# Last four steps of a Mamba-2 scan beside the first gated products: the order of three engines' helper work

## Chip, cores and metric

The kernel runs on one core of a Trainium2 chip. The metric is the device time of one execution in microseconds (us): the median of the runs, and for a profiled execution also its span, from the first to the last instruction. Engines: TensorE (PE) multiplies, VectorE (DVE) and ScalarE (ACT) work elementwise, GpSimd (POOL) too, SyncE (SP) issues transfers.

## What is computed

One macaron block over 2048 tokens of width 512: half a quantised feed-forward with a LoRA part, a Mamba-2 layer followed by a gated MLP, half a feed-forward again. The part that matters here:

```python
x = x + 0.5 * ffn(layernorm(x))
res = h0 = layernorm(x)
h = res + mamba2(rmsnorm(h0, ln1_w), ...)        # scan over 16 chunks of 128 tokens, 4 heads
#   per chunk: att = (C @ B.T) * Ldec;  Y = att @ Xdt + C @ state * exp(cs) + D * x
#              state = exp(cs[-1]) * state + dec_end * B.T @ Xdt
#              y = Y * silu(z);  y @ w_out.T
h2 = rmsnorm(h, ln2_w)
mlp = (silu(h2 @ gate_w.T) * (h2 @ up_w.T)) @ down_w.T      # inner width 1792
x = x + h + mlp
x = x + 0.5 * ffn(layernorm(x))
```

## The kernel before

The program is written by hand for every engine; each runs its own list in order, and semaphores (`wait_ge`, `then_inc`) join them. Tokens are cut into 16 chunks of 128, named c here; CH is 4, so the last four scan steps are c = 12 to 15 (`3 * CH` to `3 * CH + 3` in `late_steps`, one such function on each of GpSimd, ScalarE and VectorE). The MLP's inner width is cut into 7 pairs of 256 columns.

**TensorE in step c** (L2452 on, `step`): the transposes of the next chunk, the chunk's diagonal product with S (L2391, waits for GpSimd's e_SD), the product with the state (L2401), two more for the next step, then one gate-and-up product (`gate_up`, 24 matmuls of 128x512 at L2295), then the output product `w(c)` (L2418, L2422, L2425). Gate products are numbered n = 0 to 7; n = 0 to 3 lie in steps 12 to 15. After step 15 come n = 4, with `bound_turn(1)` (L2466) between its two halves, `bound_spread(1)` (L2471), n = 5, `down(0)` (four products t = 0 to 3), n = 6, `down(1)`, n = 7, and then seven-product units (a Strassen scheme) for pairs 1 to 6. Product n = 4 overwrites the banks of n = 3 and waits for e_gated 4, VectorE's second gate instruction of n = 3 (L2119). The product t = 3 of `down(0)` overwrites a bank that holds the bounds and waits for e_wscale 2, which VectorE gives when pair 1's scales are made. The first unit's product IP6 waits for e_gated 8 (n = 7).

**ScalarE**: `high_y` (L885) copies y to its high half; `renorm` (L875) makes n1; `gate_a` (L1376) is the tanh of a gate; `gate_b` (L1381) the high half of a gated tile; `hi2(c)` (L870) the normed high half of chunk c, into the single buffer h2n_p, so that it waits for the transpose of chunk c - 1 (s_h2T) and for GpSimd's r2 (e_rms2); `square` (L889) sums squares; `t_his` (L1325) takes high halves of the Strassen sums; `norm` (L1276) folds pair 1's scales in, waiting for e_wscale; `st_a` (L1285 to L1293) makes its high halves.

**VectorE**: `gate_y` (L1649), `low_y` (L1658), `lo2(c)` (L1596, then SyncE transposes h2n_p, L484), `t_los` (L1787) the low halves of the sums, `gate_up` (L2118, L2119), `residual2` (L1674), `gate_lo` (L2125), `bound_g` (L1708) and `bounds` (L1712 to L1715) for pair 1's maxima, `bound_row` (L1722, L1723), `scale_read` and `scales` (L1730, L1499 to L1502, L1736).

**GpSimd**: `scan_c` (L612), `scan_d` (L616, L618), `rms2(c)` (L622, L586 and the accumulating transfer L625), and `sums(first, end)`: elementwise sums of 128x512, eight for each quarter q of the tokens (n // 8 is q). They are held in four buffers hn, h2n, n0_p, hn_p (called t1, t3, t2, t4). A sum of quarter q that overwrites one of them waits (`t_ready`) until VectorE has taken the low half of that buffer's sum of quarter q - 1 (e_tlo). After the sums of q = 2 come four adds `s_adds(1)` (L774 to L779), which wait for `norm`.

The rows of an execution name these lines; in the changed file all lines behind GpSimd's list stand 5 lower, so that L1376 is L1371 there.

Of the kernel before, what the change touches and what calls it, by code (L numbers as in the profile page):

```python
# [29 lines left out]
def build(nc, x_in, w_in_t, conv_w, conv_b, a_log, d_skip, dt_bias, w_out_t, ln1_w, ln2_w,  # L30
# [14 lines left out]
    CH = ST // P  # L45
# [8 lines left out]
    with ctx:  # L54
# [522 lines left out]
        def _(po):  # L577
# [29 lines left out]
            def scan_c(c, j):  # L607
                cols = slice(j * P, (j + 1) * P)
                s = (c // CH) % 2
                po.wait_ge(e_ecs, c + 1)  # L610
                po.wait_ge(e_G, c + 1)
                po.tensor_tensor(xbc[s][:, 2:CB, cols], xbc[s][:, 2:CB, cols], ecs[:, j % 2, :, :], ALU.mult).then_inc(e_Cdec, 1)  # L612
# [83 lines left out]
            def late_steps():  # L696
                for c in range(2 * CH, 2 * CH + 3):
                    scan_c(c + 1, (c + 1) % CH)
                    scan_d(c + 1, (c + 1) % CH)
                    rms2(c, c % CH)  # L700
                scan_c(3 * CH, 0)
                scan_d(3 * CH, 0)
                rms2(2 * CH + 3, 3)
                sums(0, 2)
                scan_c(3 * CH + 1, 1)
                scan_d(3 * CH + 1, 1)
                sums(2, 4)
                rms2(3 * CH, 0)
                scan_c(3 * CH + 2, 2)
                scan_d(3 * CH + 2, 2)  # L710
                sums(4, 6)
                rms2(3 * CH + 1, 1)
                sums(6, 8)
                scan_c(3 * CH + 3, 3)
                scan_d(3 * CH + 3, 3)
                sums(8, 11)
                rms2(3 * CH + 2, 2)
                sums(11, 16)
                rms2(3 * CH + 3, 3)
                sums(16, 20)  # L720

            def sums(first, end):
                for n in range(first, end):
                    t_op(n // N_TOP, n % N_TOP)
# [108 lines left out]
        def _(ac):  # L833
# [242 lines left out]
            def late_steps():  # L1076
# [82 lines left out]
                high_y(c)  # L1159
                scan2(c + 1, 2)  # L1160
                cs_rows(c + 2)
                t_his(0, 0)
                hi2(c - 1, 0)
                gate_a(0, 1)
                renorm(c)
                gate_b(0, 1)
                square(c, 1)

                c = 3 * CH + 2
                scan_ecs(c + 1, 3)  # L1170
                scan1(c + 1, 3)
                scan_decay(c + 1, 3)
                high_y(c)
                t_his(0, 1, 2, 3)
                hi2(c - 1, 1)
                renorm(c)
                gate_a(0, 2)
                gate_b(0, 2)
                square(c, 2)

                c = 3 * CH + 3
                high_y(c)
                hi2(c - 1, 2)
                renorm(c)
                t_his(1, 0)
                gate_a(0, 3)
                gate_b(0, 3)
                square(c, 3)
                t_his(1, 1, 2, 3)

            def prologue():
                conv_pre(0)
# [134 lines left out]
            def t_his(q, *rows):  # L1327
                for r_ in rows:
                    t_hi(q, r_)
# [145 lines left out]
        def _(ve):  # L1475
# [313 lines left out]
            def t_los(q, *rows):  # L1789
                for r_ in rows:  # L1790
                    t_lo(q, r_)
# [164 lines left out]
            def late_steps():  # L1956
# [83 lines left out]
                scan1(c + 1, 2)  # L2040
                low_y(c)
                dn_lo(0)
                t_los(0, 0)
                gate_up(0, 1)
                residual2(c, 1)
                gate_lo(0, 1)
# [4 lines left out]
                scan1(c + 1, 3)  # L2051
                low_y(c)
                lo2(c - 2)
                t_los(0, 1, 2)
                gate_up(0, 2)
                residual2(c, 2)
                gate_lo(0, 2)

                c = 3 * CH + 3
                gate_y(c, 3)  # L2060
                low_y(c)
                t_los(0, 3)
                lo2(c - 2)
                bound_g(1, 0)
                bound_g(1, 1)
                gate_up(0, 3)
                bounds(1)
                residual2(c, 3)
                gate_lo(0, 3)
                lo2(c - 1)  # L2070
                bound_row(1)
                t_los(1, 0, 1, 2, 3)
# [696 lines left out]
```

## Time and profile before

| | us |
|---|---|
| median of 3 runs | 754.52 (754.46 to 755.45) |
| profiled execution | 754.62 |
| its span | 752.9 |
| busy TensorE / VectorE / ScalarE / GpSimd | 738.4 / 636.7 / 456.0 / 343.0 |

TensorE is busy for 98% of the span; the page also gives its granted clock in 40 slices, and all but a few stand at 9 or more tenths. The last four scan steps lie at about 270 to 313 us of the span. A share of busy time doesn't say what a stage is worth; for that one reads which waits of TensorE remain, and what ended last before each.

### The profile page before, as it was taken

The numbers are of one execution on the slowest core, as the hardware profiler recorded it, in microseconds if no ns is written. First come the engines' busy times: TensorE is split into PE (matmuls) and PEld (weight loads), VectorE is DVE, ScalarE is ACT, GpSimd is POOL, SyncE is SP. The second block draws the span as 40 slices with busy tenths as digits, with TensorE's granted clock in tenths as the row PEclk, the third lists the DMA queues.
The fourth block names the chain that finished last, engine by engine and source line by source line (L and its number), as shares of the span: only waits on it lengthen the run. The fifth ranks groups of instructions, "written<-read, shape, count | busy, mean of one in ns | idle before, by whom it ended". The sixth has DMA issues, their size and how long they took to land.

```text
span 752.9 us, 10655 instructions
## 1 busy us (share of the span) xinstructions
PE 738.4 (98%) x3424; PEld 360.2 (48%) x3424; DVE 636.7 (85%) x1257; ACT 456.0 (61%) x895; POOL 343.0 (46%) x391
## 2 busy tenths in 40 slices
PE   8999999999999999699999999999999999999998
PEld 3444455555555565344444444444444444444444
DVE  7799999889989997668899977977977978767994
ACT  4868888787787777345546456357356456444441
POOL 5632455665453478776423243243242243214574
PEclk9999999999999999899999999999999999999999
DMA  8933666564431224240612734734734633434474
GB/s 299 202 76 77 165 100 126 115 139 99 98 85 43 44 69 114 56 112 1 154 29 42 169 56 89 164 56 84 168 57 79 160 70 71 84 71 77 117 170 140
DMA packets 98790, 77.67 MB, mean 103 GB/s; under 512 B 65600, under 2 KB 73088, under 8 KB 98736
## 3 DMA queue, kind: packets, MB, share of 16 engines
q0 software_dynamic: 17280, 31.46, 23.6%
q1 hardware_dynamic: 78592, 41.01, 20.9%
q10 hardware_dynamic: 2864, 4.52, 2.0%
q8 instruction: 28, 0.46, 0.3%
q14 instruction: 26, 0.21, 0.1%
HBM read 24.77 MB, written 5.54 MB: 40 GB/s over the span
## 4 chain that ended last, share of the span: by engine, by line
PE 58%; DVE 26%; ACT 7%; issue 4%; DMA 3%; POOL 1%; ACTq 0%; DVEq 0%; POOLq 0%
PE PS L2295 56%; DVE raw L1683 3%; DVE st L1505 2%; DVE stage L1683 2%; DVE S L1640 2%; DVE h2n_p L1596 1%; DMA x_t<-hb 1%; DVE state L1665 1%; DVE xs L1604 1%; DVE w_in L1575 1%; DMA h<-h2n_p 1%; DVE hn_p L1584 1%; DVE stage L1691 1%; ACT Ld L929 1%; DVE raw L1691 1%
## 5 line engine op out<-in xcount | busy, mean ns | idle before, releaser
L2295 PE MATMUL PS<-h,w_in 128*128 128x512 f16 x480 | 108.1, 379 | 0.0
L2295 PE MATMUL PS<-h,x_t 128*128 128x512 f16 x408 | 95.9, 384 | 5.7 <-DVE PS L2119 5.6
L790 POOL DMA_DIRECT2D xs<-x x42 | 36.3, 871 | 92.4 <-ACT x L1368 91.6
L2295 PEld LDWEIGHTS PS<-h,w_in 128*128 128x128 f16 x480 | 46.4, 98 | 61.5 <-issue 10.1
L2295 PE MATMUL PS<-n_T,stage 128*128 128x512 f16 x288 | 71.5, 379 | 0.0
L2295 PEld LDWEIGHTS PS<-h,x_t 128*128 128x128 f16 x408 | 39.7, 99 | 55.4 <-DVE PS L2119 6.0
L1368 ACT ACTIVATE x<-PS,d_d 128x512 f32<-128x512 f32 x59 | 40.2, 682 | 39.4 <-PE PS L2295 36.6
L586 POOL TENSOR_TENSOR r<-mv,mhalf 128x1 f32<-128x1 f32 (+1 forms) x32 | 28.9, 904 | 52.2 <-DVE mv L1509 38.4
L1338 ACT ACTIVATE xds<-tm,dgh 128x512 f32<-128x512 f32 x24 | 17.3, 722 | 53.3 <-DVE tm L2219 53.3
L2295 PE MATMUL PS<-pre,stage 128*128 128x512 f16 x192 | 49.3, 379 | 0.0
L2295 PEld LDWEIGHTS PS<-n_T,stage 128*128 128x128 f16 x288 | 28.1, 98 | 34.0 <-ACT x L1368 0.3
L2295 PE MATMUL PS<-w_ffn,raw_gu 128*128 128x512 f16 (+1 forms) x204 | 43.3, 366 | 0.0
L790 POOL DMA_DIRECT2D xl<-x x17 | 14.7, 863 | 59.9 <-ACT x L1368 46.4
L790 POOL DMA_DIRECT2D xs<-n x21 | 18.3, 870 | 39.2 <-ACT n L1368 35.8
L2295 PE MATMUL PS<-w_in,x_t 128*128 128x512 f16 x144 | 34.8, 379 | 0.0
L2295 PE MATMUL PS<-raw,x_t 128*128 128x512 f16 x144 | 34.7, 379 | 0.0
L2295 PE MATMUL PS<-h,n 128*128 128x512 f16 x144 | 33.4, 379 | 0.3 <-DVE S L2188 0.3
L1368 ACT ACTIVATE n<-PS,d_d 128x512 f32<-128x512 f32 x29 | 19.8, 683 | 22.2 <-PE PS L2295 22.2
L2295 PEld LDWEIGHTS PS<-w_ffn,raw_gu 128*128 128x128 f16 x204 | 19.9, 98 | 21.8 <-DMA raw_gu<-h2n_p 0.3
L1683 DVE SCALAR_TENSOR_TENSOR raw<-pre,cw,raw 128x512 f32<-128x512 f32 x36 | 27.6, 767 | 2.9 <-ACT raw L989 2.6
L2295 PEld LDWEIGHTS PS<-pre,stage 128*128 128x128 f16 x192 | 18.8, 98 | 22.7 <-ACT x L1368 0.3
L2295 PE MATMUL PS<-w_ffn,n_T 128*128 128x512 f16 x120 | 27.5, 379 | 0.0
(349 smaller groups left out, 1884.8 us busy)
## 6 DMA issues: line engine op xcount, KB each, us to landing
xs<-x POOLq DMA_DIRECT2D x58, 256.0 KB, 3.3
xs<-n POOLq DMA_DIRECT2D x21, 256.0 KB, 3.2
xl<-x POOLq DMA_DIRECT2D x17, 256.0 KB, 3.3
x_t<-x_in SPq DMA_DIRECT2D x16, 256.0 KB, 3.5
x_t<-hb POOLq DMA_DIRECT2D x16, 256.0 KB, 4.8
out<-x_t SPq DMA_DIRECT2D x15, 256.0 KB, 2.3
raw_gu<-gate_t SPq DMA_DIRECT2D x7, 512.0 KB, 4.4
raw_gu<-up_t SPq DMA_DIRECT2D x7, 512.0 KB, 6.4
```

The lines of the kernel that those rows point to most:

```text
L586: return po.tensor_tensor(dst, src, mhalf[:, 0:src.shape[-1]], ALU.pow)
L790: po.dma_start(end_row(c), d_tmps[d % 3], accum_op=ALU.add).then_inc(s_acc[d % 3], 16)
L929: last = ac.activation(Ld[:, h, :], rows_of(j)[:, h, :], ACT.Abs, bias=ncs[:, s, j * H + h:j * H + h + 1])
L1338: ac.activation(th_s[ab], u4 if ab else c11, ACT.Tanh, scale=dgh[:, p % 2:p % 2 + 1]).then_inc(e_tanh_g, 1)
L1368: ac.activation(d_tmps[d % 3], bank(d_bank(d)), ACT.Copy, scale=d_d[:, p % 3:p % 3 + 1]).then_inc(e_ev, 1)
L1505: chain(ve.bn_stats(stat, src))
L1575: last = ve.scalar_tensor_tensor(w_in[1][:, k, piece], raw_in[:, k, piece], lsw[:, k:k + 1], w_in[0][:, k, piece], ALU.mult, ALU.subtract)
L1584: return ve.tensor_tensor(pair_[:, 1, :], src, pair_[:, 0, :], ALU.subtract)
L1640: last = ve.scalar_tensor_tensor(S[:, s, h, :], heads(B_G)[:, h, :], dt[:, (c // CH) % 2, j * H + h:j * H + h + 1], Ld[:, h, :], ALU.mult, ...
L1683: ins = ve.scalar_tensor_tensor(xbc[i % 2][:, b, :], pre[:, w, k:k + ST], cw[:, b, k:k + 1], xbc[i % 2][:, b, :], ALU.mult, ALU.add)
L1691: ve.scalar_tensor_tensor(xbc[i % 2][:, b, :], th[:, 0, :], 1.0, xbc[i % 2][:, b, :], ALU.add, ALU.mult).then_inc(e_xbc, 1)
L2295: ins = pe.matmul(out_, lhs(a, b, k), rhs(a, b, k), start=first and n == 0, stop=last and n == len(todo) - 1)
```

## The change

Only orders change, and one kind of wait is added. In step c of 12 to 15:

- ScalarE takes the gate's tanh and `gate_b` (in step 15 also renorm) ahead of `hi2(c - 1)`, and `t_his` in other places.
- VectorE takes fewer `t_los` ahead of the gates; `bounds(1)` goes ahead of gate 3; `lo2(13)` moves up into step 14.
- GpSimd waits in each step for e_y (VectorE's `gate_y`), then makes two sums, then `scan_c` and `scan_d` of the next step, then `rms2` of the step before. Its sums 8 to 15 go behind `rms2(14)`, where 8 to 10 stood ahead of it.

```diff
@@ gpsimd late_steps
-                sums(0, 2)
-                scan_c(3 * CH + 1, 1)
-                scan_d(3 * CH + 1, 1)
-                sums(2, 4)
-                rms2(3 * CH, 0)
-                scan_c(3 * CH + 2, 2)
-                scan_d(3 * CH + 2, 2)
-                sums(4, 6)
-                rms2(3 * CH + 1, 1)
+                for c in range(3 * CH, NCH - 1):
+                    po.wait_ge(e_y, c + 1)
+                    sums(2 * (c - 3 * CH), 2 * (c - 3 * CH) + 2)
+                    scan_c(c + 1, (c + 1) % CH)
+                    scan_d(c + 1, (c + 1) % CH)
+                    if c > 3 * CH:
+                        rms2(c - 1, (c - 1) % CH)
                 sums(6, 8)
-                scan_c(3 * CH + 3, 3)
-                scan_d(3 * CH + 3, 3)
-                sums(8, 11)
                 rms2(3 * CH + 2, 2)
-                sums(11, 16)
+                sums(8, 16)
                 rms2(3 * CH + 3, 3)
                 sums(16, 20)
@@ scalar late_steps, c = 3 * CH + 1, + 2, + 3
-                t_his(0, 0)
-                hi2(c - 1, 0)
                 gate_a(0, 1)
                 renorm(c)
                 gate_b(0, 1)
                 square(c, 1)
+                t_his(0, 0)
+                hi2(c - 1, 0)
...
-                t_his(0, 1, 2, 3)
-                hi2(c - 1, 1)
                 renorm(c)
                 gate_a(0, 2)
                 gate_b(0, 2)
+                hi2(c - 1, 1)
                 square(c, 2)
+                t_his(0, 1, 2)
...
-                hi2(c - 1, 2)
                 renorm(c)
-                t_his(1, 0)
+                t_his(0, 3)
                 gate_a(0, 3)
                 gate_b(0, 3)
+                hi2(c - 1, 2)
                 square(c, 3)
-                t_his(1, 1, 2, 3)
+                t_his(1, 0, 1, 2, 3)
@@ vector late_steps, c = 3 * CH + 1, + 2, + 3
-                t_los(0, 0)
...
-                t_los(0, 1, 2)
+                t_los(0, 0)
                 gate_up(0, 2)
                 residual2(c, 2)
                 gate_lo(0, 2)
+                lo2(c - 1)
...
-                t_los(0, 3)
-                lo2(c - 2)
                 bound_g(1, 0)
                 bound_g(1, 1)
+                bounds(1)
+                t_los(0, 1)
                 gate_up(0, 3)
-                bounds(1)
                 residual2(c, 3)
                 gate_lo(0, 3)
+                t_los(0, 2, 3)
                 lo2(c - 1)
```

**ScalarE, step 15, before** (split is y's high half, h2n_p a normed half, n1 renorm, th the tanh, stage `gate_b`, junk the square, w_in0 a high half of the sum named on its right):

```order
L885 ACTIVATE split<-PS 128x512 [waits e_wo,e_y]
L870 ACTIVATE h2n_p<-x2,r2 128x512 [waits s_h2T,e_rms2]
L875 ACTIVATE n1<-xs,b1,r1 128x512 [waits e_x2]
L1325 ACTIVATE w_in0<-hn 128x512 [waits e_T]
L1376 ACTIVATE th<-PS,dgh 128x512 [waits e_descale,e_gu]
L1381 ACTIVATE stage<-PS 128x512 [waits e_gated]
```

and in the change:

```order
L880 ACTIVATE split<-PS 128x512 [waits e_wo,e_y]
L870 ACTIVATE n1<-xs,b1,r1 128x512 [waits e_x2]
L1320 ACTIVATE w_in0<-hn_p 128x512 [waits e_T]
L1371 ACTIVATE th<-PS,dgh 128x512 [waits e_descale,e_gu]
L1376 ACTIVATE stage<-PS 128x512 [waits e_gated]
L865 ACTIVATE h2n_p<-x2,r2 128x512 [waits s_h2T,e_rms2]
```

The normed half, with its wait for a transpose, has gone from ahead of the tanh to behind `gate_b`.

**VectorE, step 15 from `low_y` on, before** (w_in1 a low half, mk and mx3 the bounds, th and PS the gate, x2 the residual, mr `bound_row`):

```order
L1658 TENSOR_TENSOR raw_r<-PS,split 128x4x128 [waits e_y_hi]
L1787 TENSOR_TENSOR w_in1<-hn_p,w_in0 128x512 [waits e_thi]
L1596 SCALAR_TENSOR_TENSOR h2n_p<-x2,r2,h2n_p 128x512 [waits e_h2_hi]
L1708 TENSOR_REDUCE mk<-raw_gu 128x4 [waits s_raw]
L1708 TENSOR_REDUCE mk<-raw_gu 128x4
L2118 SCALAR_TENSOR_TENSOR th<-th,PS 128x512 [waits e_tanh_g]
L2119 SCALAR_TENSOR_TENSOR PS<-th,PS 128x512 [waits e_silu_g]
L1712 TENSOR_REDUCE mx3<-raw_d 128x1
```

and in the change, up to the low half of hn_p:

```order
L1703 TENSOR_REDUCE mk<-raw_gu 128x4
L1707 TENSOR_REDUCE mx3<-raw_d 128x1
L1709 TENSOR_TENSOR mk<-mk,ln2 128x8 [waits e_mk]
L1710 TENSOR_REDUCE mx3<-mk 128x2 [waits e_dve]
L1782 TENSOR_TENSOR w_in1<-h2n,w_in0 128x512 [waits e_thi]
L2113 SCALAR_TENSOR_TENSOR th<-th,PS 128x512 [waits e_tanh_g]
L2114 SCALAR_TENSOR_TENSOR PS<-th,PS 128x512 [waits e_silu_g]
L1669 TENSOR_TENSOR x2<-n1,PS 128x512 [waits s_acc1,e_wo,e_n1]
L2120 TENSOR_TENSOR stage<-PS,stage 128x512 [waits e_gated_hi]
L1782 TENSOR_TENSOR w_in1<-n0_p,w_in0 128x512 [waits e_thi]
L1782 TENSOR_TENSOR w_in1<-hn_p,w_in0 128x512 [waits e_thi]
```

The low half of h2n (quarter 0), taken in step 14 before, now stands behind all bounds, and those of n0_p and hn_p behind the gate.

**GpSimd from `scan_d(15)` on, before** (S is `scan_d`, hn to hn_p the sums, ms, r2 and xs are `rms2`):

```order
L618 TENSOR_TENSOR S<-S,d_diag 128x512
L736 TENSOR_TENSOR hn<-h2 128x512
L736 TENSOR_TENSOR h2n<-h2 128x512
L750 TENSOR_TENSOR hn<-h2n,hn 128x512
L622 TENSOR_SCALAR ms<-ssq 128x1
L586 TENSOR_TENSOR r2<-ms,mhalf 128x1
L625 DMA xs<-x2 128x512
L736 TENSOR_TENSOR n0_p<-h2 128x512
```

and in the change, from the transfer of `rms2(13)` on:

```order
L625 DMA xs<-x2 128x512
L731 TENSOR_TENSOR hn_p<-h2 128x512
L760 TENSOR_TENSOR hn_p<-n0_p,hn_p 128x512
L622 TENSOR_SCALAR ms<-ssq 128x1
L586 TENSOR_TENSOR r2<-ms,mhalf 128x1
L625 DMA xs<-x2 128x512
L731 TENSOR_TENSOR hn<-h2 128x512
L731 TENSOR_TENSOR h2n<-h2 128x512
L745 TENSOR_TENSOR hn<-h2n,hn 128x512
L731 TENSOR_TENSOR n0_p<-h2 128x512
```

The last two sums of quarter 0 and `rms2(14)` now stand ahead of the eight sums of quarter 1.

## Rows read from the trace of the kernel before

**Rows 1.** What TensorE waited for from 264 to 405 us: total, times, longest
```profile
PE PS L2295 <- DVE PS L2119: 5.6, 1, 5.6
PE PS L2391 <- POOL S L618: 0.7, 1, 0.7
```

**Rows 2.** TensorE in order of time: start, length, line, operands, [idle before <-releaser]
```profile
291.01 1.02 PE L2391 MATMUL PS<-S,tm 128*128 128x512 f32 x2
...
305.35 5.34 PE L2295 MATMUL PS<-h,x_t 128*128 128x512 f16 x24
...
312.36 1.07 PE L2425 MATMUL PS<-split,raw_r 128*128 128x512 f32 x4
319.04 4.60 PE L2295 MATMUL PS<-h,x_t 128*128 128x512 f16 x12 [5.61 <-DVE PS L2119]
...
331.77 5.34 PE L2295 MATMUL PS<-n_T,stage 128*128 128x512 f16 x24
...
356.37 1.46 PE L2295 MATMUL PS<-w_in,raw 128*128 128x512 f16 x6
```

**Rows 3.** Stretches: length, busy PE, PEld, DVE, ACT, POOL, PEclk, DMA share, GB/s
```profile
302.58:313.43 10.85, 10.09 (x46) 5.88 (x46) 8.87 (x10) 3.09 (x6) 10.37 (x11) 1.00 0.20 50
313.43:319.04 5.61, 0.00 (x1) 0.01 (x1) 2.44 (x4) 2.55 (x5) 2.26 (x2) 0.73 0.20 46
319.04:323.64 4.60, 4.60 (x14) 1.77 (x15) 3.19 (x6) 2.85 (x6) 1.71 (x3) 0.59 0.04 10
```

**Rows 4.** ScalarE in order of time
```profile
315.01 0.72 ACT L870 ACTIVATE h2n_p<-x,r 128x512 f16<-128x512 f32 x1 [7.15 <-DMA h<-h2n_p]
...
334.57 3.30 ACT L1276 ACTIVATE raw_gu<-raw_gu,lsw 128x256 f32<-128x256 f32 x8 [3.11 <-DVEq L1737]
...
343.71 0.61 ACT L1293 ACTIVATE raw<-stage 128x512 f16<-128x512 f32 x1
```

**Rows 5.** VectorE in order of time
```profile
282.77 0.75 DVE L1649 SCALAR_TENSOR_TENSOR PS<-PS,d_ih,raw 128x512 f32<-128x512 f32 x1
...
308.50 1.97 DVE L1787 TENSOR_TENSOR w_in<-hn_p,w_in 128x512 f16<-128x512 f32 x1
...
312.09 2.33 DVE L1708 TENSOR_REDUCE mk<-raw_gu 128x4 f32<-128x1024 f32 x2
...
318.28 0.69 DVE L2119 SCALAR_TENSOR_TENSOR PS<-th,PS 128x512 f32<-128x512 f32 x1
318.89 1.21 DVE L1712 TENSOR_REDUCE mx<-raw_d 128x1 f32<-128x1024 f32 x1
...
324.24 0.67 DVE L1787 TENSOR_TENSOR w_in<-hn,w_in 128x512 f16<-128x512 f32 x1
...
330.93 0.84 DVE L1499 TENSOR_SCALAR mxa<-mxa 128x3 f32<-128x3 f32 x1
331.81 0.17 DVE L1500 TENSOR_SCALAR pw<-mxa 128x3 int32<-128x3 int32 x1
...
333.37 1.11 DVE L1736 TENSOR_TENSOR lsw<-sw,ln 128x8 f32<-128x8 f32 x1
...
355.35 0.69 DVE L2119 SCALAR_TENSOR_TENSOR PS<-th,PS 128x512 f32<-128x512 f32 x1
```

**Rows 6.** GpSimd in order of time
```profile
288.56 2.15 POOL L618 TENSOR_TENSOR S<-S,d_diag 128x512 f32<-128x512 f32 x1
...
321.85 0.46 POOL L622 TENSOR_SCALAR ms<-ssq 128x1 f32<-128x1 f32 x1 [6.08 <-ACT junk L889]
...
325.06 2.67 POOL L736 TENSOR_TENSOR hn<-h 128x512 f32<-128x512 f16 x1 [1.25 <-DVE w_in L1787]
...
335.65 1.27 POOL L765 TENSOR_TENSOR hn_p<-n_p,hn_p 128x512 f32<-128x512 f32 x1
...
337.95 1.29 POOL L774 TENSOR_TENSOR w_in<-raw_gu 128x512 f32<-128x512 f32 x1 [1.03 <-ACT raw_gu L1276]
...
341.77 1.27 POOL L779 TENSOR_TENSOR stage<-raw_gu,w_in 128x512 f32<-128x512 f32 x1
```

## The prediction, made before the changed kernel was run

> **What bounds the kernel now.** I read first what TensorE waits for in and behind the last scan steps, then its own timeline, then the engine that releases it. From 264 to 400 us it waits twice [rows 1]: 5.6 us for the second gate instruction of n = 3, and 0.7 us for `scan_d(15)`. All else there is back to back. The long wait stands ahead of n = 4, whose first 12 matmuls then take 4.60 us [rows 2]. At full clock 24 take 5.18 from one block's start to the next (5.34 less the overlap), so 12 take 2.59: the wait costs another 2.0 us. The granted clock shows why: 1.00 ahead of the gap, 0.73 in it, 0.59 behind it [rows 3], that is 1.2 GHz for part of the time, after 5.6 us without work. From 1.00 and 0.50, 0.73 says that it fell some 2.6 us into the gap. So 5.61 + 0.70 + 2.0 = 8.3 us are lost in this stage. The cause is ScalarE: `hi2(14)` stood 7.15 us waiting for the transpose of chunk 13 [rows 4], with renorm, a sum's high half and the tanh queued behind it.
>
> **What the change removes.** The tanh no longer stands behind a transpose. Gate product n = 3 begins at 304.65 if the 0.70 is gone too: GpSimd's two sums move ahead of `scan_c(15)`, but start at y's copy, and three are no longer in the way. It ends at 310.0, tanh 0.7 and two gate instructions of 0.7 each make it 312.3 at best. TensorE is done with w(15) at 313.43 - 0.70 = 312.7 [rows 2], so nothing would be waited for. But VectorE must be free. In its new order: gate_y from 304.7 to 305.4 if `lo2(13)`, now ahead of it, is not held (it can be, below), y's high half on ScalarE 0.6, low_y 0.6, bound_g 2.3 to 309.4, bounds 1.4 to 310.8 [rows 5], the low half of h2n to 311.4, and the two gate instructions to 312.8. I take 0.2 us of waiting, with 0 and 1.3 as bounds (0.67 against 1.97 for one low half [rows 5]). n = 4 then starts at 312.9 for 319.04, and at full clock: 6.1 + 2.0 = 8.1 us ahead.
>
> **The wait for y in GpSimd.** What is queued behind it are two sums and `scan_c`, `scan_d`; TensorE waits for the latter. In step 13 gate_y starts at 282.77 [rows 5], the sums take 2.5, scan_c 1.3, the select and the add with d_diag begin when S is there (288.56 before [rows 6]) and are done at 289 to 290.7; TensorE wants it at 291.01 [rows 2]. In step 15 it gives about 300.9 against 302.6. So it costs nothing; if the y copy were 1.5 us later it would begin to cost.
>
> **What is late next.** Before, GpSimd made quarter 1's sums with no one in the way and then idled 6.08 us [rows 6]. Now its second sum of quarter 1 overwrites h2n and must wait for that buffer's low half, which VectorE takes at 311.4, behind the bounds; the fourth waits for n0_p's low half, behind the gate: 312.8 + 0.75 (residual2) + 0.6 (gate_lo) + 0.6 = 314.8. From there five sums of 1.25 [rows 6] and `rms2(15)` remain, and `hi2(15)`, `lo2(15)`, gate n = 4 and the scales are queued behind them on their engines (ScalarE's four high halves and VectorE's four low halves of quarter 1 stand ahead). Unhindered the five sums end at 321.1. They are not unhindered: VectorE's low halves and GpSimd's sums hold each other up. A low half of 0.67 took 1.97 beside a sum, and a sum of 1.27 took 2.67 beside low halves [rows 5, 6]. I count three such meetings (quarter 0's last low half with `lo2(14)`, and quarter 1's first two) of about 1 us each, by the half-way point between 0 and 1.4: 324.2. Then ms and r2 0.9, so `hi2(15)` at 325.1; lo2(15) meets a sum, 327.6; gate n = 4 1.4, 329.0; the scales, which took 3.7 from reading to the end at 334.48 [rows 5], until 332.8.
>
> TensorE arrives at t = 3 of `down(0)`, which waits for these scales, at 331.77 + 3 x 1.295 - 8.1 = 327.5. **It waits 5.3 us**, nearly as long as before, and for that the clock falls again: 2.0 us. At t = 3 it is 335.66 - 332.8 = 2.9 ahead, after the slow stretch 0.9; rounded down for the 0.1 of restarting, 0.8.
>
> A second path ends at the first unit's IP6, which starts at 356.37 when e_gated 8 is there at 355.35 + 0.72 = 356.07 [rows 2, 5]: only 0.3 us of slack. It comes from GpSimd's adds for pair 1, over ScalarE's last high half at 343.71 [rows 4, 6]. Before, quarter 2's eight sums took from 325.06 to 336.92, of which 1.4 is the first one's being held; the four adds then waited for `norm` until 337.95 and ended at 343.04. Now quarter 2 starts behind rms2's transfer at 325.8, takes 10.4 + 0.6 for one meeting, 336.8, and the adds follow at once (norm ends at 332.8 + 3.4), four times 1.27, until 341.9. That is 1.1 ahead. So TensorE, 0.8 ahead, sets the end of this stretch, and VectorE and GpSimd are just in time.
>
> Behind that the units keep TensorE busy with the same work, so 0.8 us is what reaches the end: the profiled 754.62 becomes 753.8, and its median, 0.1 below it, 753.7.
>
> **A rule of the Trainium skill beside this.** The rows show scale instructions over 3 to 8 columns at 0.84 and 1.11 us beside running sums, and one of 0.17 between [rows 5]. The Trainium skill (SBUF — State Buffer, "SBUF: two separate sides") says that VectorE and GpSimd share a pair of ports as an exclusive lock, held for a whole instruction, not a split of bandwidth. By that rule each meeting costs up to one sum, and the scales keep their 3.7 us wherever sums run; with a split, the group would be some 2.5 us shorter (an estimate from the 0.17 row), and the time 2 to 3 us lower. The rows speak for the lock.
>
> **Rivals.**
> - *The new wait is short.* If only one of the three meetings costs, the scales are there at 330.8: wait 3.3, clock probably falls, 4.9 - 2.0 = 2.9 ahead; the adds are 3.1 ahead. Time 751.6. With no meeting at all, and none in the adds, the second path gives 5.2 ahead, 749.3. For it: most low halves in the trace take 0.67 [rows 5]. Against: in this stretch both engines work off the same four buffers in turn.
> - *The whole gain stays.* If the scales didn't depend on quarter 1's sums, 8.3 less: 746.2. Against it stands the program's order on three engines.
> - *Slower.* VectorE can take low halves back to back and keep GpSimd out through all of them: at 324.24 four followed each other at 0.67, and the sum beside them took 2.67 [rows 5, 6]. Here the run would be two low halves, lo2(14), the bound's row and hn's low half, so that the fourth sum starts at 317.7 rather than 315.8: 1.9 us later than I count, or 2.4 with one more meeting. The scales come at 335.2, TensorE is 0.5 ahead at t = 3 and, with the slow clock, 1.5 behind; the second path gives 1.3 behind. Time 756.1. It decides from where the scales come later than 335.66 - 2.0 = 333.7, which is 0.9 later than my value.
> - *The change doesn't do what it says:* another transpose could keep the tanh back. renorm needs only x2 of the step before, and no h2n_p instruction stands ahead of the last tanh. I give it nothing of its own.
>
> **How the numbers follow.** Forecast (the gap moves to t = 3, 752.9 to 755.0) 0.55; short wait 0.25; whole gain 0.05; slower 0.15. A measurement of this kernel tells 0.2%, 1.5 us, from no change: below 753.0 is faster, above 756.0 slower. All of the whole gain, four fifths of the short wait and a little of the forecast are faster: 0.29. Of the slower case half passes 756.0, and of the forecast a small tail: 0.12. The rest, 0.59, is no change. The range reaches into both neighbours, from 751.0 to 756.0; 749.3 and 746.2 lie outside.
>
> **What the profile of the changed kernel would show.** TensorE's row of n = 4 without an idle time of over 1 us, and its 12 matmuls at 2.6 to 2.8. No wait for scan_d. A new wait of 4 to 6 us inside down(0), released by VectorE's scales, with a granted clock of about 0.5 behind it. GpSimd idle for 2 to 4 us ahead of the second or fourth sum of quarter 1, released by a low half, and no longer idle ahead of rms2(15). ScalarE idle ahead of quarter 1's last high half in place of the normed halves. The adds of pair 1 ending at 341 to 343. If down(0) shows no wait, the prediction is wrong by the chain through GpSimd; if the clock stays at 1.00 behind it, by 2 us; if IP6 waits, the second path sets the time.

## Result, and the profile after

| | before, us | change, us |
|---|---|---|
| median of 22 runs each | 755.12 | 752.91 |
| profiled execution, its span | 754.62, 752.9 | 752.58, 750.8 |

The ratio is 0.9974, with a 95% interval of 0.9965 to 0.9983: 0.26% faster, 2.0 to 2.2 us, where 0.8 to 0.9 was forecast. It lies in the range, and on the side of faster, which had less of the chances than no change. The changed kernel's trace lies 0.54 us late against the one of before from some 200 us on, ahead of all that the change touches (TensorE's product with S of step 14 starts at 291.55 beside 291.01 in [rows 2]); times of before and of the prediction are compared below with that added.

What TensorE waited for from 264 to 405 us (total, times, longest), to be read against [rows 1]:

```profile
PE PS L2290 <- DVEq L1732: 3.9, 1, 3.9
PE PS L2290 <- DVE PS L2114: 0.5, 1, 0.5
PE PS L2290 <- DVE S L2183: 0.3, 1, 0.3
```

TensorE in order of time, against [rows 2]:

```profile
311.73 1.07 PE L2420 MATMUL PS<-split,raw_r 128*128 128x512 f32 x4
313.32 2.76 PE L2290 MATMUL PS<-h,x_t 128*128 128x512 f16 x12 [0.53 <-DVE PS L2114]
...
324.22 4.05 PE L2290 MATMUL PS<-n_T,stage 128*128 128x512 f16 x18
332.16 2.74 PE L2290 MATMUL PS<-n_T,stage 128*128 128x512 f16 x6 [3.89 <-DVEq L1732]
334.69 5.56 PE L2290 MATMUL PS<-h,x_t 128*128 128x512 f16 x24
340.09 5.34 PE L2290 MATMUL PS<-n_T,stage 128*128 128x512 f16 x24
...
354.34 1.46 PE L2290 MATMUL PS<-w_in,raw 128*128 128x512 f16 x6
```

The wait ahead of n = 4 is 0.53 instead of 5.61 us, its 12 matmuls take 2.76 instead of 4.60, and the 0.70 for `scan_d` is gone. The 0.3 us for S stand in the kernel before as well. In their place TensorE stands still for 3.89 us inside `down(0)`, ahead of t = 3, until the scales are there. The granted clock in stretches around that wait (length, busy PE, PEld, DVE, ACT, POOL, PEclk, DMA share, GB/s) falls as in [rows 3], from its upper level of 2.4 GHz toward the lower of 1.2:

```profile
327.00:330.00 3.00, 1.27 (x6) 0.39 (x4) 2.90 (x6) 0.60 (x1) 2.92 (x3) 1.00 0.90 304
330.00:333.00 3.00, 0.84 (x3) 0.30 (x4) 2.71 (x8) 0.86 (x3) 2.84 (x3) 0.79 1.21 217
333.00:336.00 3.00, 3.00 (x11) 1.15 (x10) 0.32 (x1) 3.00 (x8) 2.92 (x4) 0.65 0.22 45
336.00:340.00 4.00, 4.00 (x20) 1.86 (x19) 3.26 (x5) 1.43 (x4) 3.92 (x4) 1.00 0.00 0
```

From 332.16 to 340.09 are 7.93 us for 30 matmuls; at 1.295 for six, as elsewhere, they would be 6.48. The clock cost 1.45 us; over the six matmuls from 332.16 to 334.69 it was at 0.50, the lower level.

Who is late for the scales is read from GpSimd (in order of time), which idled 6.08 us ahead of `rms2(15)` in [rows 6] and now has its sums there:

```profile
312.08 1.16 POOL L731 TENSOR_TENSOR h2n<-h 128x512 f32<-128x512 f16 x1 [3.67 <-DVE w_in L1782]
313.32 1.28 POOL L745 TENSOR_TENSOR hn<-h2n,hn 128x512 f32<-128x512 f32 x1
315.30 1.53 POOL L731 TENSOR_TENSOR n_p<-h 128x512 f32<-128x512 f16 x1 [0.70 <-DVE w_in L1782]
316.91 1.59 POOL L751 TENSOR_TENSOR h2n<-n_p,h2n 128x512 f32<-128x512 f32 x1
318.58 1.66 POOL L754 TENSOR_TENSOR n_p<-n_p,hn 128x512 f32<-128x512 f32 x1
320.21 1.60 POOL L731 TENSOR_TENSOR hn_p<-h 128x512 f32<-128x512 f16 x1
321.89 1.59 POOL L760 TENSOR_TENSOR hn_p<-n_p,hn_p 128x512 f32<-128x512 f32 x1
323.57 0.19 POOL L622 TENSOR_SCALAR ms<-ssq 128x1 f32<-128x1 f32 x1
```

and from VectorE behind it, up to the scales:

```profile
319.20 1.59 DVE L1782 TENSOR_TENSOR w_in<-h2n,w_in 128x512 f16<-128x512 f32 x1
320.94 1.42 DVE L1782 TENSOR_TENSOR w_in<-n_p,w_in 128x512 f16<-128x512 f32 x1
...
325.19 1.82 DVE L1591 SCALAR_TENSOR_TENSOR h2n_p<-x,r,h2n_p 128x512 f16<-128x512 f32 x1 [0.32 <-ACT h2n_p L865]
...
331.88 0.17 DVE L1731 TENSOR_TENSOR lsw<-sw,ln 128x8 f32<-128x8 f32 x1
```

The path over the adds has room: they end at 340.70, VectorE's last gate instruction of n = 7 ends at 353.65, 0.69 us ahead of IP6, and IP6 waits for nothing.

### The profile page after: what moved, and what is told of

It is laid out like the page before. It is cut to its first block, busy times and chain, and to the rows that moved or that the text cites. A ratio compares the mean times of both kernels' runs of the same rounds, so it can differ in the third digit from the quotient of the medians.

```text
span 750.8 us, 10655 instructions
## 1 busy us (share of the span) xinstructions
PE 737.4 (98%) x3424; PEld 359.9 (48%) x3424; DVE 638.3 (85%) x1257; ACT 456.5 (61%) x895; POOL 340.9 (45%) x391
## 4 chain that ended last, share of the span: by engine, by line
PE 71%; DVE 17%; POOL 3%; issue 3%; ACT 3%; DMA 2%; ACTq 0%; POOLq 0%; DVEq 0%; SPq 0%
PE PS L2290 62%; DVE stage L1678 2%; DVE st L1500 1%; PE PS L2428 1%; DMA x_t<-hb 1%; PE PS L2420 1%; PE PS L2386 1%; DVE h2n_p L1591 1%; DVE raw L1678 1%; PE PS L2413 1%; PE PS L2404 1%; PE PS L2378 1%; PE PS L2417 1%; PE PS L2396 1%; DVE S L1635 1%
## 5 line engine op out<-in xcount | busy, mean ns | idle before, releaser
L2290 PE MATMUL PS<-h,x_t 128*128 128x512 f16 x408 | 94.3, 380 | 0.6 <-DVE PS L2114 0.5
L2290 PEld LDWEIGHTS PS<-n_T,stage 128*128 128x128 f16 x288 | 28.3, 99 | 38.8 <-DVEq L1732 4.4
L785 POOL DMA_DIRECT2D xs<-n x21 | 18.5, 880 | 39.3 <-ACT n L1363 35.6
L1363 ACT ACTIVATE n<-PS,d_d 128x512 f32<-128x512 f32 x29 | 19.8, 684 | 22.5 <-PE PS L2290 22.5
```

The source lines that it names most:

```text
L785: po.dma_start(end_row(c), d_tmps[d % 3], accum_op=ALU.add).then_inc(s_acc[d % 3], 16)
L1363: ac.activation(d_tmps[d % 3], bank(d_bank(d)), ACT.Copy, scale=d_d[:, p % 3:p % 3 + 1]).then_inc(e_ev, 1)
L2290: ins = pe.matmul(out_, lhs(a, b, k), rhs(a, b, k), start=first and n == 0, stop=last and n == len(todo) - 1)
```

## Experiments

Each kernel was timed in five rounds beside the kernel before; a ratio is against that one. "Way" is the time from the start of step 15's product with S (L2386 in the change) to the start of IP6 in the profiled execution, which leaves out where a trace begins: 51.38 us in the change, and 53.09 before (where 0.70 us of waiting for that product stand ahead of it, and 0.54 in e8). "hi2(15)" is when ScalarE starts on chunk 15's high half, "adds" when GpSimd's last add for pair 1 ends, both also counted from L2386's start. Beside the waits in the table, TensorE waits 1.35 us for `bound_row` in e3, and 0.52 us inside n = 4 in e11 and e12.

| kernel | median, us | ratio (95%) | way | waits of TensorE: n = 4 / t = 3 / n = 6 / later | hi2(15) | adds |
|---|---|---|---|---|---|---|
| change | 752.91 | 0.9974 (0.9965 to 0.9983) | 51.38 | 0.53 / 3.89 / - / - | 21.5 | 37.7 |
| e1 | 752.45 | 0.9964 (0.9952 to 0.9975) | 51.36 | 0.54 / - / 3.62 / - | 20.7 | 37.7 |
| e2 | 750.54 | 0.9944 (0.9928 to 0.9959) | 48.60 | 1.92 / 0.26 / 0.53 / - | 19.2 | 35.5 |
| e3 | 753.67 | 0.9987 (0.9974 to 1.000) | 52.97 | - / 4.03 / 0.40 / - | 22.5 | 38.8 |
| e4 | 754.71 | 1.000 (0.999 to 1.001) | 53.50 | 0.54 / - / 3.81 / 0.53 | 20.7 | 36.9 |
| e5 | 753.34 | 0.998 (0.997 to 0.9989) | 52.27 | 0.56 / 0.46 / - / 0.72, 2.35, 0.78 | 18.9 | 39.2 |
| e6 | 752.35 | 0.9969 (0.9958 to 0.998) | 51.75 | 0.45 / 3.90 / 0.24 / - | 21.4 | 37.6 |
| e7 | 749.50 | 0.9928 (0.9914 to 0.9942) | 48.62 | 0.43 / 1.51 / 0.86 / - | 19.1 | 35.4 |
| e8 | 761.07 | 1.0086 (1.0068 to 1.0103) | 59.07 | 3.02 (and 6.72 at n = 3) / - / - / - | 27.9 | 44.8 |
| e9 | 749.67 | 0.9936 (0.9924 to 0.9949) | 48.69 | 0.45 / 1.43 / - / 0.72 | 19.3 | 35.6 |
| e10 | 752.70 | 0.9974 (0.9965 to 0.9983) | 50.94 | 0.55 / 0.47 / - / 0.73, 1.10, 2.07 | 17.9 | 36.8 |
| e11 | 749.48 | 0.9931 (0.9919 to 0.9944) | 48.40 | 0.42 / - / - / 1.79 | 15.1 | 35.3 |
| e12 | 747.47 | 0.9907 (0.9892 to 0.9922) | 46.70 | 0.44 / - / - / - | 15.1 | 32.4 |

**Two paths end at IP6.** It starts when TensorE is done with what lies ahead of it and when VectorE's last gate instruction of n = 7 is there. In all traces but e4's, VectorE begins `st_a` 1.3 us behind the last add. From there to the end of that gate instruction it takes 11.65 us, 0.66 of them idle for ScalarE, unless `st_a` itself is held up, and IP6 follows 0.14 us later at the earliest. So "adds" + 13.1 is the earliest IP6. For the change that is 50.8, below its way of 51.38: TensorE's own path ends last. For e2, e7, e9 and e11 it is 48.6, 48.5, 48.7 and 48.4, against ways of 48.60, 48.62, 48.69 and 48.40, and for e5 52.3 against 52.27: there the adds end last, or tie. This sum was read from the traces afterwards; no expectation below used it.

**The parts of the change.** e3 is the change with GpSimd's list of before, e8 the kernel before with GpSimd's list of the change.

> The changed kernel with GpSimd's list of the kernel before: the GpSimd part of the change undone. Theory A: the third sum of quarter 1 stands ahead of rms2(14), so rms2(14) waits with it for h2n's low half at 312 us, the fourth sum starts 0.9 us later, scan_d(15) keeps TensorE waiting for 0.5 to 0.7 us again: 0.9 to 1.6 us slower than the changed kernel, still 0.5 to 1.3 us faster than before. Theory C (GpSimd's order is what made the gain): as slow as before or slower.

> The kernel before with only GpSimd's new list (operands tied to y's copy, sums two a step), ScalarE's and VectorE's lists as before. Theory A (the parts of the change only pay together: ScalarE's high half 3 of quarter 0 then waits for sums that GpSimd does behind the last scan operand, and chunk 13's and 14's halves and gates wait behind it): 0.7 to 1.5 us slower than the kernel before, 755.8 to 756.6. Theory B (GpSimd's list alone brings what the change brings): 753 to 754.

e3 is 0.8 to 1.0 us above the change, as its first theory said, though the two intervals overlap. The place was another: `scan_d(15)` keeps TensorE waiting for nothing, and it waits 1.35 us for `bound_row` (L1723), which stands behind chunk 14's halves and so behind `rms2(14)`. Against the kernel before, e3's interval reaches 1.000, so its other theory, as slow as before, isn't ruled out. For e8 the first theory had the right sign and was far too small, 6.3 us slower against 0.7 to 1.5. ScalarE in e8 (in order of time) shows why:

```profile
308.48 0.63 ACT L1320 ACTIVATE w_in<-hn_p 128x512 f16<-128x512 f32 x1 [7.98 <-POOL hn_p L760]
309.02 0.70 ACT L865 ACTIVATE h2n_p<-x,r 128x512 f16<-128x512 f32 x1
309.63 0.80 ACT L870 ACTIVATE n<-xs,b,r 128x512 f32<-128x512 f32 x1
310.33 0.67 ACT L1371 ACTIVATE th<-PS,dgh 128x512 f32<-128x512 f32 x1
```

The old list asks for the last high half of quarter 0 ahead of gate n = 2's tanh, and GpSimd's new list makes that sum only behind `scan_d(15)`. Chunk 13's high half, renorm and the tanh hang on it: TensorE waits 6.72 us ahead of n = 3. ScalarE's and VectorE's lists alone bring 0.13% or nothing, GpSimd's alone costs 0.86%, together they bring 0.26%; the two can't be priced one by one.

**GpSimd's wait for y.** e6 leaves it out.

```diff
                 for c in range(3 * CH, NCH - 1):
-                    po.wait_ge(e_y, c + 1)
```

> The change without GpSimd's wait for y's copy ahead of the last scan steps' operands. Theory A (the wait costs nothing, since scan_d(14) ends 0.5 us before TensorE wants it and GpSimd has slack there): within 0.4 us of the change, 752.5 to 753.3. Theory B (the 4.64 us in which GpSimd waits there push its sums and so the end): 1.5 to 4 us faster than the change.

0.9969 against 0.9974: no difference that these runs can tell, though the median lies 0.15 us below the range that was named. GpSimd's 4.64 us of idle time there cost nothing that shows. Most of it comes back elsewhere in e6: GpSimd waits 3.3 us for ScalarE's operand of the scan (L914), and 4.3 us instead of 2.3 for VectorE's S.

**What the wait at t = 3 is worth.** e1 makes the scales as soon as GpSimd and VectorE allow, ahead of quarter 1's last three low halves.

```diff
@@ vector, end of late_steps
-                t_los(1, 0, 1, 2, 3)
+                t_los(1, 0)
+                scale_read(1)
+                scales(1)
+                descale(1)
+                t_los(1, 1, 2, 3)
@@ and behind gate n = 4
-            scale_read(1)
-            scales(1)
-            descale(1)
```

> The changed kernel with one edit on VectorE: reading pair 1's bounds, its scales and descale stand behind the first low half of quarter 1, ahead of the other three, where in the changed kernel they stand behind all four, lo2(15) and gate n = 4. Theory A (two paths end in this stretch: the scales that down(0)'s t = 3 waits for, and GpSimd's adds of pair 1, which end at 340.7 us in the changed kernel and set e_gated 8 at 353.7, 0.7 us ahead of IP6's start at 354.34): the 3.9 us wait at t = 3 and the slow clock behind it (1.5 us) go, but a new wait stands ahead of IP6 or of down(1), and only 0.3 to 1.0 us reach the end. Theory B (the wait at t = 3 alone sets the time): 5.3 us less than the changed kernel, 0.7% more.

The wait is gone and the time is the same, 0.5 us less by the medians with intervals that overlap. The first theory had the size, but looked for the next wait ahead of IP6 or `down(1)`. TensorE in e1:

```profile
324.64 5.34 PE L2291 MATMUL PS<-n_T,stage 128*128 128x512 f16 x24
333.61 7.04 PE L2291 MATMUL PS<-h,x_t 128*128 128x512 f16 x24 [3.62 <-DMA h<-h2n_p]
```

Gate n = 6, one step on, needs chunk 15 transposed, and `lo2(15)` is late by the same chain: 3.62 us of waiting and 1.7 of clock (7.04 for 5.34). So two waits of about one length lay over one another, and the second showed only when the first was gone.

**The adds ahead of quarter 2's last four sums.** e4 is e1 with this:

```diff
             late_steps()
+            s_adds(1)
             sums(2 * N_TOP + 4, 3 * N_TOP)
-            s_adds(1)
```

> e1_scales_early with a second edit, on GpSimd: the four adds of pair 1 stand ahead of the last four sums of quarter 2. Theory A: norm ends at about 332 us, the adds run from 332.4 to 337.5 (340.7 in the changed kernel), e_gated 8 comes near 351, and the time is 2.5 to 3.3 us below the changed kernel; what stays of a wait stands ahead of down(1) (1.5 to 2 us, for VectorE's first accumulation). Theory B: no more than e1 gave.

It missed by 4.3 to 5.1 us, to the slow side. The adds wait for `norm`, which stands on ScalarE behind gate n = 4, and that behind `lo2(15)`: it ended at 335.16 and not at 332. GpSimd stood still for 4.26 us and had the sums still to do when VectorE came to `st_a`. VectorE in e4:

```profile
342.09 2.78 DVE L1763 TENSOR_TENSOR raw<-w_in,raw 128x256 f16<-128x256 f32 x2
344.79 1.75 DVE L1764 TENSOR_TENSOR raw<-stage,raw 128x512 f16<-128x512 f32 x1
```

These took 0.76 and 0.69 in the change. The adds end 0.8 us earlier than there, and VectorE's way from `st_a` to the gate instruction takes 14.76 us instead of 11.65; that sets IP6. TensorE comes late too, since the clock cost 3.0 us behind its wait at n = 6 (e1: 1.7), and so IP6 waits only 0.53 us. Whatever is to bring the adds forward must bring `norm` forward first.

**Quarter 0's low halves.** GpSimd's 3.67 us of idle time ahead of its second sum is a wait for a low half that stands on VectorE behind 3.7 us of bounds. e2 turns them round, and e7 puts `bounds(1)` behind the gate on top:

```diff
@@ vector, step 15, e2
+                t_los(0, 1, 2)
                 bound_g(1, 0)
                 bound_g(1, 1)
                 bounds(1)
-                t_los(0, 1)
                 gate_up(0, 3)
                 residual2(c, 3)
                 gate_lo(0, 3)
-                t_los(0, 2, 3)
+                t_los(0, 3)
@@ and e7
-                bounds(1)
                 gate_up(0, 3)
+                bounds(1)
```

> The changed kernel with one edit on VectorE in step 15: the low halves of h2n and n0_p of quarter 0 stand ahead of the bounds of pair 1, so that GpSimd's second to sixth sum of quarter 1 need not wait for them (they began at 312.1 and 315.3 us). Theory A (GpSimd's sums of quarter 1 are the chain behind both paths): gate n = 3 comes 1.3 us later and TensorE waits about 1.9 us ahead of n = 4 at full clock, but the quarter's sums end 4 us earlier, t = 3 waits for nothing, the adds end 4 us earlier, and the time is 3 to 4 us below the changed kernel. Theory B (what counts is the gap ahead of n = 4): 1.4 us slower than the changed kernel.

> The kernel that does quarter 0's first three low halves ahead of the bounds (750.54 us), with the bounds moved on, behind the gate of the next step. Theory A (TensorE's 1.92 us wait at gate n=4 there is for VectorE's queue, in which the bounds, about 1.5 us, stand ahead of what it wants): the wait falls to about 0.5 us, but 0.4 to 1.4 us of it come back as waits at down(0) t=3 or at gate n=6, since chunk 15's chain isn't moved: 749.5 to 750.5. Theory B (the wait is the whole price): 748.6 to 749.1.

e2 is 2.3 us faster than the change, less than the 3 to 4 of its first theory. The 1.92 us at n = 4 had been named; but quarter 1's sums and the adds come 2.2 to 2.3 us earlier and not 4, one of the sums taking 2.87 us beside three low halves in a row:

```profile
318.12 2.87 POOL L760 TENSOR_TENSOR hn_p<-n_p,hn_p 128x512 f32<-128x512 f32 x1
```

e7 takes 1.5 of them, of which 1.25 at t = 3 and 0.3 at n = 6 come back in its trace; its ratio is 0.16% below that of e2, and the two intervals overlap. The way is the same in both, 48.60 and 48.62, with the adds at 35.5 and 35.4. e7's median lies in the range of its first theory. Both wait at t = 3 and n = 6 for chunk 15 still.

**Chunk 15 ahead of quarter 1's sums.** In e5 GpSimd does chunk 15's sum of squares after three of quarter 1's sums, with ScalarE's and VectorE's lists to match; e10 puts the adds two sums forward on top.

```diff
@@ gpsimd
-                sums(8, 16)
+                sums(8, 11)
                 rms2(3 * CH + 3, 3)
+                sums(11, 16)
@@ vector: t_los(1, 0, 1) in late_steps, then lo2(15), gate n = 4, scales, and
+            t_los(1, 2)
             gate_lo(0, EARLY_GU)
+            t_los(1, 3)
@@ gpsimd, e10
-            sums(2 * N_TOP + 4, 3 * N_TOP)
+            sums(2 * N_TOP + 4, 2 * N_TOP + 6)
             s_adds(1)
+            sums(2 * N_TOP + 6, 3 * N_TOP)
```

> The change, with chunk 15's normed tile ready earlier: GpSimd does three of quarter 1's remaining sums, then chunk 15's scan sum of squares, then the other five; ScalarE and VectorE halve chunk 15 and open gate n=4 right behind it, the last two halves of quarter 1 follow behind that gate. Theory A (one cause stands behind all three ends of the last stage: GpSimd's quarter-1 sums ahead of chunk 15's sum of squares, so its transpose for the 6th gate matmul, its scales and its norm all come late): the 3.89 us wait of TensorE at down(0) t=3 shrinks under 0.5 us and no wait at gate n=6 takes its place, the granted clock stays 1.00 there; but quarter 2's sums still run as late as before, so only 0.7 to 1.5 us come off against the change: 751.4 to 752.2. Theory B (the wait for the scales sets the end, and all of it is worth its 3.9 + 1.45 us): 747 to 748. Theory C (quarter 1's last halves come too late for down(1), and the gain is lost): no change to 1 us slower than the change.

> The kernel with chunk 15 ahead of quarter 1's last five sums (753.34 us), and on top GpSimd's four adds two sums of quarter 2 earlier. In the kernel without it the adds began at 336.97 us though the norm was done at 332.40, and TensorE then waited 0.72, 2.35 and 0.78 us. Theory A (these waits are the adds' path, pushed 1.8 us by the 1.38 us in which GpSimd waited for a low half queued behind the scales): the adds begin near 334.5 and end near 340 us, 2 of the 3.9 us of waits go: 750.5 to 751.7. Theory B (the waits come from VectorE's queue, not from the adds): 752.8 to 753.8.

e5 did at t = 3 and n = 6 what was expected and was yet 0.4 to 0.5 us slower than the change by the medians, with intervals that overlap: the third theory, the gain lost. TensorE in e5:

```profile
336.50 5.35 PE L2295 MATMUL PS<-n_T,stage 128*128 128x512 f16 x24 [0.72 <-DVE xl L2137]
...
352.08 2.74 PE L2295 MATMUL PS<-n_T,stage 128*128 128x512 f16 x6 [2.35 <-DVE xs L2137]
355.60 1.46 PE L2295 MATMUL PS<-w_in,raw 128*128 128x512 f16 x6 [0.78 <-DVE PS L2117]
```

A low half of quarter 1 now stood behind the scales, GpSimd's quarter 2 waited 1.38 us for it, the adds ended 1.5 us later than in the change (39.2 beside 37.7), and VectorE, which takes `st_a` ahead of `down(1)`'s results, was late with all that follows. In e10 the adds end 2.4 us earlier, and 1.3 us of way come back; by the medians it is 0.4 to 0.6 us, with intervals that overlap. The first theory, 750.5 to 751.7, was missed. The rows show where the other 1.0 us went: a sum that now stands behind the adds meets `st_a`, as in e4. VectorE in e10:

```profile
340.84 1.77 DVE L1767 TENSOR_TENSOR raw<-w_in,raw 128x256 f16<-128x256 f32 x2 [2.43 <-ACT raw L1290]
```

That is 1.77 us instead of 0.76, and VectorE's way to the gate instruction is 12.67 instead of 11.65. TensorE's three waits behind 330 us don't shrink, 3.90 us in all beside 3.85; the slow clock behind the wait of 2.35 us, which cost 1.3, is what is gone.

**All three, and the floor below.** e9 is e7 with chunk 15 early, its sum of squares in the 0.78 us in which GpSimd idled ahead of quarter 1's last two sums.

```diff
-                sums(8, 16)
+                sums(8, 14)
                 rms2(3 * CH + 3, 3)
+                sums(14, 16)
@@ scalar and vector: the halves (1, 3) go behind gate n = 4 and the scales
```

> The kernel with quarter 0's low halves ahead of the bounds and the bounds behind the gate (749.5 us), and chunk 15 early on top: GpSimd does its sum of squares in the 0.78 us in which it waits there, ahead of the last two of quarter 1's sums; ScalarE and VectorE halve chunk 15, open gate n=4 and make the scales ahead of quarter 1's last halves. Theory A (one cause, GpSimd's sums ahead of chunk 15's sum of squares, stands behind the two waits that are left, 1.51 us at down(0) t=3 and 0.86 us at gate n=6; quarter 2's sums begin no later than before, so the path over the adds isn't pushed): both waits go, nothing comes in their place, 2.0 to 2.8 us faster: 746.7 to 747.5. Theory B (the path over quarter 2's sums and the adds takes over at once, as it did where chunk 15 went ahead of five sums and cost 0.9 us): within 0.5 us of 749.5, and TensorE waits for VectorE's st_a or gate parts behind 340 us.

A miss of the first theory: no gain over e7. The second had the time and the path: the adds end at 35.6, and IP6 starts 0.14 us behind the gate instruction. What it said of the waits was wrong, since TensorE comes to IP6 only 0.3 us ahead of its operand: it is held up before, 1.43 us at t = 3 and 0.72 at `down(1)`. ScalarE in e9:

```profile
322.43 0.72 ACT L866 ACTIVATE h2n_p<-x,r 128x512 f16<-128x512 f32 x1 [4.62 <-DMA h<-h2n_p]
```

What held chunk 15 was no longer GpSimd. There is one buffer h2n_p, and its transposing transfer for chunk 14 was issued as VectorE's low half ended (316.61 + 0.74 = 317.35) and landed 5.0 us later. That low half stood behind the bounds, the residual and two other halves. In the change, e2, e7, e11 and e12 the same transfer lands in 2.7 us; in e5, e9 and e10, where `rms2(15)`'s transfer is issued 0.4 us behind it, in 5.2, 5.0 and 3.3. So moving that sum of squares forward may itself have slowed the transpose; no run separates the two. The theory "one cause, GpSimd's sums" fell here; e11 tests the next one, the buffer, by halving chunk 14 earlier.

```diff
@@ scalar, step 15
                 gate_a(0, 3)
+                hi2(c - 1, 2)
                 gate_b(0, 3)
-                hi2(c - 1, 2)
@@ vector, step 15
                 gate_up(0, 3)
+                lo2(c - 1)
                 bounds(1)
                 residual2(c, 3)
                 gate_lo(0, 3)
                 t_los(0, 3)
-                lo2(c - 1)
```

> The kernel with all three moves (749.67 us), and on top chunk 14 halved earlier: its high half between the two gate parts of ScalarE (the engine waits there 2.44 us), its low half ahead of VectorE's bounds. There the high half of chunk 15 waited 4.62 us for the transposing transfer of chunk 14, which reads the only h2n_p buffer and landed 5.0 us behind VectorE's low half. Theory A (this buffer is the floor under chunk 15's chain, and the path over the adds is a second one that ties with it: VectorE was busy without a gap from 339 us to gate n=8's part at 351.7 us, 0.1 us ahead of TensorE): chunk 15's high half starts 2.5 to 3.4 us earlier, the waits of 1.43 us at down(0) t=3 and 0.72 us for xl go, and some 2 us come back as one wait for a gate part near 350 us: 749.0 to 749.7. Theory B (the buffer is the whole price): 747.2 to 747.8.

> The kernel of the line above, and on top GpSimd's four adds of S ahead of the last two sums of quarter 2. Theory A (the buffer and the adds are the two floors, and both are moved now): the adds end 2 to 3 us earlier than in the kernel above, the wait near 350 us goes, 747.0 to 748.2. Theory B (the last two sums, pushed behind the adds, meet VectorE's st_a halves, as they did where the adds went ahead of four sums and st_a's halves took 2.78 and 1.75 us): 748.8 to 750.

Both came out by their first theory. In e11 chunk 15 starts 4.2 us earlier (2.5 to 3.4 expected), TensorE runs through from n = 5 to n = 7 with no wait, and a wait comes back where it was named, 1.79 us ahead of IP6, so that the time is that of e9. TensorE and, below it, the last of VectorE's instructions ahead of it in e11:

```profile
347.35 1.46 PE L2293 MATMUL PS<-n_T,stage 128*128 128x512 f16 x6
350.60 1.46 PE L2293 MATMUL PS<-w_in,raw 128*128 128x512 f16 x6 [1.79 <-DVE PS L2116]
```

```profile
333.44 1.58 DVE L1759 TENSOR_TENSOR n<-raw_gu,n 128x512 f16<-128x512 f32 x1
338.80 0.76 DVE L1765 TENSOR_TENSOR raw<-w_in,raw 128x256 f16<-128x256 f32 x2 [3.78 <-ACT raw L1289]
...
349.76 0.69 DVE L2116 SCALAR_TENSOR_TENSOR PS<-th,PS 128x512 f32<-128x512 f32 x1
```

The 3.78 us ahead of `st_a` are the adds. With the adds ahead of quarter 2's last two sums (e12) they end 2.9 us earlier and the wait goes:

```profile
347.41 1.46 PE L2294 MATMUL PS<-n_T,stage 128*128 128x512 f16 x6
348.95 1.46 PE L2294 MATMUL PS<-w_in,raw 128*128 128x512 f16 x6
```

The move brings 2.0 us by the medians and 1.7 of way; in e10 it brought 0.4 to 0.6 and 1.3 of way. By the traces the two are nearly alike, 2.4 and 2.9 us on the adds less what `st_a` loses to a sum. VectorE in e12:

```profile
335.96 1.94 DVE L1766 TENSOR_TENSOR raw<-w_in,raw 128x256 f16<-128x256 f32 x2 [0.76 <-ACT raw L1290]
```

32.4 + 13.1 + 1.2 = 46.7 is e12's way. e12 is the fastest of all, 0.9907 (0.9892 to 0.9922), 7 us below the kernel before. Was e11's move needed for it? In e9 TensorE comes to IP6 0.27 us ahead of its operand, so by its trace the adds alone could have brought no more than that; in e11 it is 1.95. No run has e9 with the adds moved.

## Why the prediction was right, and where its sizes were off

- **n = 4.** Right. It starts at 313.32, predicted 312.9 (313.4 with the offset); it waits 0.53 where 0.2 was taken, between bounds of 0 and 1.3, and its matmuls run at full clock. The 8.1 us are there. The terms named for `bound_g`'s end add up to 308.9 and not 309.4, but the trace has 309.94, 309.4 without the offset: `lo2(13)` did hold gate_y, by 0.35 us, which the prediction had left open. The slip did no harm, by luck.
- **GpSimd's wait for y.** Right: scan_d(14) ends at 291.06, TensorE starts on it at 291.55 without a wait, and e6 finds no price.
- **The new chain.** Right as to who waits for whom, and to 0.1 us as to when: the second sum starts at 312.08 behind h2n's low half (predicted 311.4 + 0.54), the fourth at 315.30 behind n0_p's (314.8 + 0.54).
- **The five sums: mis-sized.** They took 8.2 us and not 9.4. I had three meetings with low halves at 1.0 us each, "the half-way point between 0 and 1.4", which is 0.7: with that the sums take 8.4 us, and the forecast would have been 1.7 to 1.8 us and a median of 752.8. The rows show five meetings at 0.32 to 0.45: VectorE's instruction comes in the middle of a sum and waits for its end (1.59 and 1.42 us instead of 0.67), and GpSimd then waits only for what is left of a low half. So the count was too low and the price too high; that 3 times 0.7 comes near the 1.9 us measured would have been luck. The sum of 2.67 us in [rows 6], from which the 1.4 was read, stood beside the last of four low halves in a row.
- **The scales.** 3.8 us from reading to ready beside running sums, predicted 3.7; the split of bandwidth that it weighed would have taken some 2.5 us less by its estimate. With the sums 1.2 us shorter they come at 332.05, not 333.34. TensorE waits 3.89 and not 5.3, just below the 4 to 6 that the prediction would see.
- **The clock.** 1.45 and not 2.0 us. The 2.0 had been carried over from the gap of 5.61 us. That this one is shorter doesn't explain the difference: 3.81 us in e4 cost 3.0. What sets the size stays open.
- **The sum.** IP6 starts at 354.34, which with the offset is 2.57 us ahead of 356.37, forecast 0.8: 1.3 from the scales and 0.5 from the clock make up the difference. The span shows 2.1 us of it, since the offset stays in it.
- **The second path.** Quarter 2 starts at 325.04 and its sums met nobody for long (10.56 us), so the adds end at 340.70, not 342.4; IP6's gate part is ready 0.69 us ahead. It was not the end, as forecast; but with less than 0.7 us of room it ends last in e2, e7, e9 and e11.
- **The rivals.** The result lies between the forecast and the short wait, and the range was wide enough for both: the mechanism was right at each wait that the change's trace shows, the 0.8 us were not. The rival that ended slower needed VectorE to keep GpSimd out through a run of two low halves, `lo2(14)`, the bound's row and hn's low half. That run was there, but it didn't keep GpSimd out: the fourth sum started at 315.30, `lo2(14)` beside it took 1.64 us, and the later low halves came one by one, as their sums were made. In e2 a run of three low halves did keep a sum waiting, 2.87 us.
- **Missed altogether:** that gate n = 6 waits for chunk 15's transpose as long as t = 3 waits for its scales (e1), and that h2n_p's single buffer holds chunk 15 next, 2 us below GpSimd's chain (19.3 in e9 against 21.5 in the change, from L2386's start), where the transfer takes 5.0 us. The trace of before shows the buffer: it is the 7.15 us of [rows 4]. The prediction removed that wait and didn't ask where the same buffer would hold next. Neither changes the number for this change. They and the adds decide what "the whole gain" would have taken: e12 has five moves, and still ends some 8.3 - 7 = 1.3 us short of it, with waits of 0.44 and 0.52 us at n = 4 and 0.24 at IP6 left.

What stays open: why chunk 14's transfer took 5.0 us in e9 and 3.3 in e10, and what sets the loss by the clock.

## What to carry to other kernels

When a long wait goes, look for all that its chain feeds, not for the next reader alone. Here the scales, a transpose and the adds were late by one chain. Making the scales early brought nothing that shows (e1), the adds on top a loss (e4), scales and transpose together nothing (e5); moving what held the chain, GpSimd's wait for two low halves, brought 2.3 us at once (e2), and all moves together 5. Give each path to the same point a sum of its own: with "adds + 13.1" at hand and the adds unmoved, it could have been told ahead that e7, e9 and e11 bring next to nothing over e2. A single buffer between two engines and a transfer is worth a line of its own in the sum: the second half's end, plus the transfer's time to landing, is the earliest start of the next half. Where two paths tie, an edit on one shows nothing until the other has been moved as well: e11 alone brought 0.3 us of way, and with the adds 2.0.

## What the runs showed of the hardware

- **One side of a meeting pays more.** A VectorE instruction over 128x512 (0.67 to 0.82 us alone) that comes during a GpSimd sum took 1.42 to 1.82 us in the change, the sum after it 0.3 to 0.45 more than its 1.16 to 1.27; but three low halves in a row at 0.67 each stretched one sum to 2.87 us in e2. That agrees with the exclusive lock of which the Trainium skill speaks (SBUF — State Buffer, "SBUF: two separate sides"); which engine is next when both want it, the rows show only case by case.
- **Short waits cost no clock here, longer ones did.** TensorE's waits of 1.92, 1.51, 1.79 and 2.07 us (e2, e7, e11, e10) were followed by matmuls at full speed. After 2.35 us in e5 six matmuls took 2.74 us instead of 1.46; after 3.02 us in e8 twelve took 4.13 instead of 2.76; after 3.62 and 3.81 us (e1, e4) 24 took 7.04 and 8.31 instead of 5.34; after 3.89 in the change 1.45 us were lost. The loss isn't a fixed sum: waits that differ by 0.2 us lost 1.7 and 3.0.
- **The clock fell inside some waits and behind others.** In the kernel before it was at 1.00 over the first 2 us of the gap of 5.61 us and at 0.50 over the last 2.6. In e1 and e6 it stood at 1.00 through waits of 3.62 and 3.90 us and fell only in the busy stretch behind them (0.75 over the next 6.9 us in e1; 0.92, then 0.78 in e6).
- **A transposing transfer took 2.7 to 7.9 us for the same work.** From issue to landing, chunk 14's took 2.7 in the change and 5.0 in e9, with `rms2(15)`'s transfer issued 0.4 us behind it. Chunk 15's took 4.8 to 7.9 us where the 1280 KB of parked x were issued 2.0 to 2.6 us ahead of it (7.2 in the change, 7.8 in e11), and 3.6 where they were issued 3.4 or 5.8 us ahead (e10, e1). That the other transfers are the cause is argued from these times; no run removes one.
